# Job orders of five engines, PSUM slots and identity products of a two-layer attention and convolution kernel written anew

## The reference, cut to what matters

```python
# layer 0
attn = softmax(q @ k.T / sqrt(d) + bias)              # per 8x8 window, 4 heads
x = x + proj(attn @ v)
a, b = split(w1 @ x); g = a * sigmoid(b)
x = x + leaky(conv3x3(pad(g), w2))
# layer 1
x = x + dwconv(x, cpe1)
y = layernorm(x); act_res = silu(act @ y)
t = silu(dwconv(inp @ y, dwc))                        # nine taps per channel
q, k = elu(qk @ t) + 1; v = t
kv = rope(k).T @ v;  z = 1 / (q . mean(k))
y = rope(q) @ kv * z + dwconv(v, lepe)                # nine taps per channel
x = x + out @ (y * act_res)
x = x + dwconv(x, cpe2)
x = x + fc2 @ gelu(fc1 @ layernorm(x))
```

## Time and profile before

| | us |
|---|---|
| median of 3 runs | 854.25 |
| lowest and highest of them | 850.33, 855.42 |
| the profiled execution's own time | 852.0 |
| its span, first to last instruction | 850.2 |
| PE, DVE, ACT, POOL busy in it | 761.1, 547.1, 496.7, 299.2 |
| mean granted clock of TensorE | 0.943 of full speed |

### The profile page before, as it was taken

One profiled execution on the slowest core, in us unless ns is written; L12 is line 12 of the kernel. 1 busy time (PEld: TensorE's weight loads), 2 busy tenths in 40 slices (PEclk: granted clock), 3 DMA queues, 4 the chain that ended last, 5 costly groups with the idle time before them and its releaser, 6 DMA issues. The chain is left out here.

```text
span 850.2 us, 19878 instructions
## 1 busy us (share of the span) xinstructions
PE 761.1 (90%) x8514; PEld 478.3 (56%) x8514; DVE 547.1 (64%) x698; ACT 496.7 (58%) x675; POOL 299.2 (35%) x215
## 2 busy tenths in 40 slices
...
PEclk9899999999989996989899999999789998896999
...
GB/s 60 46 3 1 30 58 1 2 2 15 2 2 43 55 17 1 16 15 16 1 26 33 43 29 1 30 15 3 15 15 29 30 1 29 15 1 1 30 15 43
DMA packets 34345, 16.77 MB, mean 20 GB/s; under 512 B 27120, under 2 KB 34160, under 8 KB 34258
## 3 DMA queue, kind: packets, MB, share of 16 engines
...
q10 hardware_dynamic: 1808, 0.22, 0.2%
...
## 5 line engine op out<-in xcount | busy, mean ns | idle before, releaser
L1288 POOL TENSOR_TENSOR SC<-SC,mx 128x768 f32<-128x768 f32 x48 | 77.8, 1621 | 229.4 <-DVE mx L1096 229.3
L568 PE MATMUL ps<-ZP,wdw 48*64 48x384 f32 x1728 | 143.8, 483 | 1.2 <-ACT QH L990 0.8
L1163 DVE SCALAR_TENSOR_TENSOR CT<-TP,vec_sb,CT 112x768 f32<-112x768 f32 x96 | 130.2, 1368 | 1.3
L1149 DVE SCALAR_TENSOR_TENSOR QS<-ZP,vec_sb,QS 112x768 f32<-112x768 f32 x96 | 109.3, 1163 | 0.6
L568 PEld LDWEIGHTS ps<-ZP,wdw 48*64 48x64 f32 x1728 | 66.2, 133 | 72.2 <-issue 65.0
L1135 DVE TENSOR_TENSOR LV<-LV,XB 112x768 f32<-112x768 f32 x24 | 24.7, 1030 | 98.5 <-ACT LV L942 98.5
L659 PEld LDWEIGHTS ps<-vx,PT 128*128 128x128 f32 x576 | 71.6, 204 | 13.3 <-issue 5.9
L659 PE MATMUL ps<-vx,PT 128*128 128x52 f32 x576 | 74.2, 288 | 3.1 <-DVE KX L1170 1.2
L568 PE MATMUL ps<-G,w_sb 48*64 48x384 f32 x864 | 74.2, 494 | 1.9 <-ACT G L907 0.9
L815 PEld LDWEIGHTS ps<-ident_sb 128*128 128x128 f32 x534 | 64.7, 197 | 19.2 <-issue 12.2
L815 PE MATMUL ps<-ident_sb 128*128 128x128 f32 x534 | 71.2, 287 | 2.7 <-DVE XB L1221 1.4
...
## 6 DMA issues: line engine op xcount, KB each, us to landing
...
w_sb<-in_w_dram SPq DMA_DIRECT2D x2, 81.0 KB
...
wln_sb<-in_const_dram SPq DMA_DIRECT2D x6, 9.0 KB
```

The source lines that it names most:

```text
L568: mm = pe.matmul(slot(job)[half(c, HALF), r * BANK:r * BANK + SPX], w[half(r), tap * HALF:(tap + 1) * HALF], shifted(t, d * CROWS + c * WI ...
L1149: dve.scalar_tensor_tensor(out=rows16(T0[n]), in0=win, scalar=wt, in1=rows16(T0[n]), op0=ALU.mult, op1=ALU.add).then_inc(dwc_step, 1)
L1163: dve.scalar_tensor_tensor(out=ct, in0=win, scalar=wt, in1=ct, op0=ALU.mult, op1=ALU.add).then_inc(lepe_step, 1)
L1288: pool.tensor_tensor(sc, sc, bc_last(mx[:, (u % NSC) * 12:(u % NSC) * 12 + 12], TOK), ALU.subtract).then_inc(sub_ready, 1)
```

## The change

Only the five texts are replaced; no function, size, buffer or data changes. Every list holds the same jobs as before: 491 on PE, 444 on ACT, 481 on DVE, 108 on POOL, 54 on SP. Three things differ.

- The order. A job moves by 4 to 6 places on average on PE, ACT and DVE. On SP one pair of neighbours is swapped.
- The PSUM slots: 335 of the 491 jobs of PE write another slot.
- The identity products: 322 where there were 267, and at other jobs. Before `kv`, `kp`, `kk` of the last pair there are 109 (before: 91), ahead of its `kt.3.1` 20 of them, and ahead of `d3.3.0` 31 (before: 26).

The core of the diff (the ACT text and most lines of the others are left out):

```diff
--- before.py
+++ after.py
 PE_ORDER = """
...
-    v.0.0@0 v.0.1@1 s1.0.0@2+8 qk.0.0@3 sc0.0.0@0+11 sc1.0.0@1 qk.0.1@2 sc0.0.1@3+12 tr0.0.0@0+4 sc1.0.1@1
-    qk.0.2@2 tr1.0.0@0 av.0.0@0 v.0.2@3 sc0.0.2@2 ot.0.0@0 tr0.0.1@3+4 pj.0.0@1 sc1.0.2@0 qk.0.3@3 tr1.0.1@2
...
-    cv.0.2@1 qk.1.0@0 v.1.0@2 v.1.1@3 d0.0.0@1 sc0.1.0@0 sc1.1.0@2 qk.1.1@3 xc.0.0@1 d0.0.1@0 va.0.0@1 sc0.1.1@2
-    xc.0.1@3 tr1.1.0@0 d0.0.2@2 va.0.1@1 tr0.1.0@3 xc.0.2@0 ip.0.0@2 sc1.1.1@1 va.0.2@0 qk.1.2@2 ip.0.1@3
-    av.1.0@1 tr0.1.1@0 v.1.2@3 sc0.1.2@2 tr1.1.1@0 ot.1.0@1 ip.0.2@3 av.1.1@0 pj.1.0@1 v.1.3@3 tr0.1.2@2
...
-    sc0.3.5@1 v.3.5@0 kp.2.0@3 ot.3.3@2 cv.3.0@0 pj.3.3@1 tr0.3.4@2 tr1.3.4@3 sc1.3.5@0 kk.2.0@1 dn.2.0@2
...
-    f11.2.2@1 f2.2.2@3+5 kt.3.0@2 vt.3.0@1 q.3.0@0 kv.3.0@3+33 kt.3.1@1 vt.3.1@2 q.3.1@0 kt.3.2@3+17 vt.3.2@2
-    q.3.2@1 kv.3.1@0+4 kv.3.2@2+27 kp.3.0@3+6 kk.3.0@0+4 dn.3.0@1 dn.3.1@2 dn.3.2@3 at.3.0@0 at.3.1@1 at.3.2@0
-    op.3.0@2+8 op.3.1@3+6 d3.3.0@1+26 op.3.2@0 xc2.3.0@2+1 va2.3.0@3+4 f10.3.0@1+11 f11.3.0@0 d3.3.1@2 d3.3.2@3
-    xc2.3.1@1 f12.3.0@0 xc2.3.2@2 va2.3.1@3 f2.3.0@1 va2.3.2@0 f10.3.1@2+7 f12.3.1@1 f11.3.1@3 f2.3.1@0+10
-    f10.3.2@2 f12.3.2@3 f11.3.2@1 f2.3.2@0+5
...
+    v.0.0@0 v.0.1@1 s1.0.0@2+9 qk.0.0@3 sc0.0.0@0+13 sc1.0.0@1 qk.0.1@2 sc0.0.1@3+14 tr0.0.0@0+5 sc1.0.1@1
...
+    tr1.0.3@2 cv.0.0@3 sc0.0.5@2 av.0.3@0 tr0.0.4@1 tr1.0.4@3 v.0.5@2 ot.0.3@1 sc1.0.5@0 av.0.4@3 tr0.0.5@2
+    pj.0.3@1 qk.1.0@0+2 ot.0.4@2 v.1.0@3 tr1.0.5@1 pj.0.4@2 sc0.1.0@0 sc1.1.0@2 av.0.5@3 qk.1.1@1 v.1.1@0
+    tr0.1.0@2 ot.0.5@3 w1.0.3@0 pj.0.5@2 w1.0.4@3 sc0.1.1@2 sc1.1.1@1 tr1.1.0@0 w1.0.5@2 av.1.0@0 tr0.1.1@3
+    tr1.1.1@1 cv.0.1@2 ot.1.0@3 av.1.1@0 pj.1.0@1 cv.0.2@2 d0.0.0@3 ot.1.1@0 qk.1.2@1 v.1.2@2 pj.1.1@3 xc.0.0@0
+    d0.0.1@3 va.0.0@1 sc0.1.2@0 xc.0.1@2 d0.0.2@3 va.0.1@0 tr0.1.2@1 xc.0.2@2 v.1.3@3 ip.0.0@0 va.0.2@2
+    sc1.1.2@1 qk.1.3@2 ip.0.1@3 ac.0.0@1 ac.0.1@0 ip.0.2@3 ac.0.2@1 w1.1.0@3 sc0.1.3@2 sc1.1.3@0 qk.1.4@3
...
+    sc0.3.5@1 ot.3.3@2 kv.2.2@0 pj.3.3@3 sc1.3.5@2 v.3.5@1 kp.2.0@0 av.3.4@1 tr0.3.5@2 kk.2.0@0 dn.2.0@3 q.2.1@2
...
+    f2.2.2@2+12 kt.3.0@0 vt.3.0@3 q.3.0@1 kt.3.1@2+20 vt.3.1@3 q.3.1@0 kv.3.0@1 kv.3.1@2+37 kt.3.2@3 vt.3.2@1
+    q.3.2@0 kv.3.2@2+38 kp.3.0@3+8 kk.3.0@1+6 dn.3.0@0 dn.3.1@2 at.3.0@3 at.3.1@1 dn.3.2@0 at.3.2@3+7 op.3.0@2+1
+    op.3.1@1+6 d3.3.0@0+31 op.3.2@3 xc2.3.0@2+1 va2.3.0@1+4 f10.3.0@0+14 f11.3.0@3 d3.3.1@2 d3.3.2@1 xc2.3.1@0
+    f12.3.0@3 xc2.3.2@2 va2.3.1@1 f2.3.0@0 va2.3.2@3 f10.3.1@2+9 f12.3.1@0 f11.3.1@1 f2.3.1@3+12 f10.3.2@2
+    f12.3.2@0 f11.3.2@1 f2.3.2@3+6
...
 DVE_ORDER = """
...
-    sb1.1.0 sb0.1.1 yn.0.0 yn.0.1 sb1.1.1 qb.1.2 yn.0.2 c10.0.0 c11.0.0 ob.1.0 c12.0.0 sb0.1.2 c13.0.0 c10.0.1
...
-    c11.0.2 c12.0.1 sb1.1.3 c13.0.1 c12.0.2 ko.0.0 c14.0.1 ob.1.2 c15.0.1 qb.1.4 c13.0.2 qo.0.0 c14.0.2 x1.1.2
...
-    c20.2.1 c27.2.0 c21.2.1 c28.2.0 x1.3.3 c22.2.1 sb1.3.5 kk.2.0 c23.2.1 c24.2.1 c25.2.1 ob.3.4 az.2.0 c26.2.1
...
+    sb0.1.1 g.0.4 sb1.1.1 g.0.5 ob.1.0 ob.1.1 x1.1.0 qb.1.2 x1.1.1 sb0.1.2 yn.0.0 yn.0.1 sb1.1.2 yn.0.2 qb.1.3
+    c10.0.0 c11.0.0 c12.0.0 c10.0.1 c13.0.0 c11.0.1 g.1.0 c14.0.0 sb0.1.3 c15.0.0 g.1.1 c16.0.0 sb1.1.3 c17.0.0
...
+    c23.2.0 ko.2.2 qb.3.5 c24.2.0 qo.2.0 ob.3.3 c20.2.1 sb0.3.5 c21.2.1 ks.2.2 sb1.3.5 kp.2.0 x1.3.3 c22.2.1
+    ob.3.4 kk.2.0 c23.2.1 c25.2.0 c24.2.1 c26.2.0 az.2.0 x1.3.4 qo.2.1 qo.2.2 c27.2.0 c25.2.1 c28.2.0 c26.2.1
...
 POOL_ORDER = """
...
-    qs.2.1 su1.3.4 qs.2.2 su0.3.5 su1.3.5 ym.2.0 ym.2.1 ym.2.2 x2.3.0 x2.3.1 x2.3.2 kr.3.0 qc.3.0 qs.3.0 kr.3.1
-    qc.3.1 kr.3.2 qc.3.2 qs.3.1 qs.3.2 ym.3.0 ym.3.1 ym.3.2
...
+    qs.2.0 su1.3.5 qc.2.1 qc.2.2 qs.2.1 ym.2.0 qs.2.2 ym.2.1 ym.2.2 x2.3.0 x2.3.1 x2.3.2 kr.3.0 qc.3.0 kr.3.1
+    qc.3.1 qs.3.0 kr.3.2 qc.3.2 qs.3.1 qs.3.2 ym.3.0 ym.3.1 ym.3.2
...
 SP_ORDER = """
...
-    py.1.1 ld.2.2 ld.2.3 py.1.2 ld.2.4 ld.2.5 st.0.0 st.0.1 st.0.2 py.2.0 pz.1.0 pz.1.1 pz.1.2 ld.3.0 ld.3.1
...
+    py.1.1 ld.2.2 ld.2.3 py.1.2 ld.2.4 ld.2.5 st.0.0 st.0.1 st.0.2 pz.1.0 py.2.0 pz.1.1 pz.1.2 ld.3.0 ld.3.1
...
```

More of the change, by code:

```diff
@@ L72 @@
[L72 to L76, removed]
@@ L154 @@
-    c20.0.2 oz.0.1 c21.0.2 c22.0.2 c23.0.2 c24.0.2 c25.0.2 c26.0.2 c27.0.2 c28.0.2 am.0.2 oz.0.2 yn2.0.0 qb.2.0
-    sb0.2.0 yn2.0.1 sb1.2.0 qb.2.1 yn.1.0 sb0.2.1 yn.1.1 sb1.2.1 yn2.0.2 qb.2.2 yn.1.2 c10.1.0 c11.1.0 c12.1.0
-    ob.2.0 c13.1.0 sb0.2.2 c14.1.0 o.0.0 c15.1.0 x1.2.0 c16.1.0 c10.1.1 c17.1.0 sb1.2.2 c18.1.0 ob.2.1 qb.2.3
-    c11.1.1 c10.1.2 c12.1.1 c11.1.2 c13.1.1 x1.2.1 c14.1.1 sb0.2.3 ko.1.0 sb1.2.3 c15.1.1 qb.2.4 c16.1.1 ob.2.2
-    o.0.1 c17.1.1 c12.1.2 c18.1.1 sb0.2.4 x1.2.2 ks.1.0 c13.1.2 c20.1.0 c14.1.2 c21.1.0 c15.1.2 c22.1.0 ob.2.3
@@ new lines @@
+    c16.0.1 sb1.1.4 c17.0.1 qb.1.5 c18.0.1 x1.1.3 qo.0.0 g.1.2 c13.0.2 sb0.1.5 ks.0.0 c14.0.2 ko.0.1 c15.0.2
+    sb1.1.5 c16.0.2 ob.1.4 g.1.3 c17.0.2 qo.0.1 c18.0.2 c20.0.0 c21.0.0 c20.0.1 c22.0.0 ks.0.1 c21.0.1 c23.0.0
+    ko.0.2 c24.0.0 x1.1.4 qo.0.2 c22.0.1 c25.0.0 g.1.4 c26.0.0 ob.1.5 ks.0.2 c27.0.0 c23.0.1 c28.0.0 c24.0.1
+    c25.0.1 kp.0.0 c26.0.1 kk.0.0 x1.1.5 c27.0.1 c28.0.1 az.0.0 am.0.0 az.0.1 am.0.1 az.0.2 oz.0.0 g.1.5 c20.0.2
+    oz.0.1 c21.0.2 c22.0.2 c23.0.2 c24.0.2 c25.0.2 c26.0.2 c27.0.2 c28.0.2 am.0.2 oz.0.2 yn2.0.0 qb.2.0 sb0.2.0
```

187 lines of the change are left out of this document (94 added, 93 removed).

## The result

| | before | after |
|---|---|---|
| median | 854.84 us (4 runs, 850.33 to 855.69) | 874.11 us (4 runs, 865.68 to 878.03) |
| profiled execution, its span | 852.0, 850.2 | 874.4, 872.6 |
| granted clock in it | 0.943 | 0.935 |

The ratio is 1.022, with a 95% interval of 1.014 to 1.031. The kernel became slower, clear of the noise (whether by more or less than 2% the interval leaves open); the forecast was 844.2 us with a range up to 860.

The account below looks back on a forecast made before the run. It took PE to set the opening and convolution stages, DVE the stencil stages. Terms 13.0 - 11.1 - 2.8 + 0.9 - 1.8 - 1.4 - 0.9 - 3.7 = -7.8 against 852.0 gave 844.2 us, range 829 to 860.

Parts of the forecast that it names:

- Opening, +13.0: Before `c10.0.0`: 14 jobs of pair 1 moved ahead of `ip.0.1` cost their full PE time, 13.0 us more.
- Stencil stage 0, -11.1: The moved strips take 9.0 us off DVE, to 88.3, and its idle falls from 6.1 to 4: 11.1 us less.
- Stages 1 and 2, +0.9 and -1.4: Stencil stages 1 and 2: DVE gains 5.3 and 4.8 us of work, its idle falls to 3.8 and 4.1.
- The rival that DVE's waits keep their size: The three stencil stages keep 6.1, 8.2 and 10.3 us of DVE idle: 12.7 us more, 857; chance 0.20.
- Convolution stages, -2.8 and -1.8: Convolution stages 0 and 1: 2.8 us less if the slow stretch stays away, 1.8 less from exchanged jobs and fewer identity products.
- Up to `kt.3.0`, -0.9: Convolution stage 2 up to `kt.3.0`: projection and gate moved out, eight identity products more, 0.9 us less.
- Tail, -3.7: Last part: earlier `kt.3.1` ends a POOL wait and more identity products remove most slow stretches, 3.7 us less.
- The clock, 17 us of the sum: Fewer low-clock stretches in stages 0, 1, 2 and the tail: gains of 3.0, 4.4, 6.2 and 3.4 us.
- the first rival: Slow stretches only change places, so 10.8 us from stages 0, 1 and the tail are not gained: 855; no change, chance 0.22.
- Slower had 0.12: Chance given to a measured time over 862.8 us: 0.10 from the slower rival, 0.02 from the other cases.

Follow-up runs that it names:

- e6: Kernel before with eight attention jobs of pair 1 moved ahead of `ip.0.1` on PE, and 5.7 us of DVE work ahead of `c10.0.0`; 861.64 us, ratio 1.0087.
- e1: After's five lists for the opening and stencil stage 0, up to `at.0.0` on PE and `az.0.0` on DVE, then before's lists; 877.97 us, ratio 1.028 to before.
- e9: Kernel before with one DVE job, `x1.3.3`, moved earlier, to right behind `c20.2.1`; 852.81 us, ratio 0.998.
- e7: Kernel before with after's lists from the tail on, but before's counts of identity products from `d3.3.0` on; 856.01 us, ratio 1.0019.
- e11: Kernel before without the 91 identity products ahead of the last pair's `kv`, `kt.3.2`, `kp`, `kk`; 852.62 us, ratio 0.998.
- e4: Kernel after with 7 identity products added ahead of `av.0.0`; 873.69 us, ratio 1.021 to before.
- e5: Kernel after with 4 identity products added ahead of `tr0.0.1` and 4 ahead of `av.0.1`; 870.93 us, ratio 1.017 to before.
- e14: Kernel after with five PE jobs of pair 1 put back behind `ip.0.1` in one block; 888.0 us, ratio 1.038 to before.
- e15: Kernel after with five PE jobs of pair 1 put back behind `ip.0.1`, interleaved with ready work; 884.4 us, ratio 1.038 to before.

## Why the prediction was wrong, step by step

**Opening, +13.0: measured +30.5.** The price of the moved work was right: e6 moved 9.6 us and `c10.0.0` was 10.3 late. What failed is that nothing else was in the sum. No term stood for the clock, which the forecast only ever let improve; in e1 it is 6.6 us, in after's profile 14.3. That it got worse here is no chance of one profile: 18 to 40 us of low clock with after's lists, 7 to 10 with before's. Nor did a term stand for idle time (+3.8 in e1, +3.0 in after).

**Stencil stage 0, -11.1: -5.8.** DVE was to fall to 88.3 and fell to 90.0; its idle was to be 4 and is 7.6. The mis-sized term is the idle one, by 3.6 us. e1 (7.2) and e6 (7.8) show the same: less work for PE in a stage did not shorten DVE's waits.

**Stages 1 and 2, +0.9 and -1.4: -1.1 and +4.1.** In stage 2 DVE's work was forecast at 106.8 and is 106.8; the idle of 4.1 is 9.6. In stage 1 DVE got 99.7, not 104.9, and idled 7.0, not 3.8; two errors hid each other. The jobs came as counted; what shrank is the time of the 40 taps in that stage, taken as fixed. Their windows (DVE busy on the taps of the first kind, then on those of the second), before and then after:

```profile
329.20:437.00 107.80, 28.02 (x24) 0.88 0.05 12
329.20:437.00 107.80, 28.34 (x16) 0.88 0.05 12
```
```profile
347.40:454.10 106.70, 25.28 (x24) 0.92 0.04 10
347.40:454.10 106.70, 25.34 (x16) 0.92 0.04 10
```

That is 56.4 us in before and 50.6 in after for the same 40 taps, more than the 5.3 that were added. Over the three stages DVE idled 24.2 us, before 24.6, where 11.9 had been taken. The rival that DVE's waits keep their size thus held as a mechanism, and is worth the 12.3 us between the two (the rival said 12.7). The forecast's argument against it, that a good half of the idle lies in slow stretches, took a coincidence in time for a cause. The wait ahead of `kk.2.0` did go in after, and e9 shows what its going is worth alone: 0.2%, at the edge of the noise.

**Convolution stages, -2.8 and -1.8: -6.5 and +4.8.** The first had the full clock, as forecast; PE was busy 5.1 us less in it and idle 3.0 for 4.4. In the second PE idled 4.3 us for 1.9 and was busy 2.5 longer; `op.1.1` follows `am.1.1` after 8.6 us where it took 4.5. No term stood for that: the jobs at the border of two stages were counted, their distance was not.

**Up to `kt.3.0`, -0.9: -2.4. Tail, -3.7: -1.2.** `kt.3.1` did come early, and the idle of POOL ahead of `kr.3.1` went. It came back one chunk on:

```profile
762.83 1.00 POOL L1254 TENSOR_TENSOR KX<-KX,rope_th_sb 98x384 f32<-98x384 f32 x1
781.09 1.73 POOL L1254 TENSOR_TENSOR KX<-KX,rope_th_sb 98x384 f32<-98x384 f32 x1 [2.29 <-DVE KX L1169]
```

and `kv.3.2` was to be at 2.1 us by the clock; it took 4.1, at 1.2 GHz still, with 37 identity products ahead of `kv.3.1` and 38 ahead of itself (PE of after, answering to the earlier trace rows):

```profile
790.12 4.11 PE L742 MATMUL ps<-KX,VT 98*64 98x144 f32 x32 [3.62 <-issue]
813.07 7.19 PE L814 MATMUL ps<-ident_sb 128*128 128x128 f32 x62
820.75 1.52 PE L567 MATMUL ps<-ZP,wdw 48*64 48x384 f32 x16 [0.49 <-issue]
```

The 31 ahead of `d3.3.0` take 7.2 us and the wait behind them is still 0.5. `az.3.0` came 2.9 us sooner behind `kt.3.0` instead of 6.1, and 1.2 of it were left at the end.

**The clock, 17 us of the sum.** This is the largest gain that was booked and did not come. Low-clock time was read off one profile, put down to named waits, and booked as gain where these went. After has 114 us of low clock in its profile, before 97; stretches of 27.3 and 17.1 came where none over 17 had been forecast. That is the first rival, the stretches change places: its mechanism held, and its price of 10.8 left out the 6.2 of stencil stage 2. The long stretches of before do belong to its order, since they recur in eleven profiles; but where they would lie in a new order the old profile could not tell. Others can be there or not with the same jobs (e7), e11 shows that taking cover away costs nothing in the tail, and by the fit a us lost is worth 0.62.

The Trainium skill (TensorE: Matmul & The Clock Gate, section What's actually happening), on which that rival drew, holds that the count of cold products varies between runs. e7 agrees, with 0.78 for 1.00 in before's profile of the same window; the long stretches do not vary that way. Its figure of under 1% of a typical kernel's span is for the ramp penalty, and the forecast held it against the clock of the whole kernel. For that it is no bound: before loses 52.0 us, at 0.62 some 32 us, 4% of 853.

**The chances.** Slower had 0.12, and its largest case was 857, less than the 862.8 from which the forecast counts a kernel as slower. Adding that rival's 12.3 us and the opening's idle and clock of e1 (3.8 and 6.6) to 844.2 gives 867, 7 us short of the measured 874. The first was a rival, with too small a chance; the other two had no term at all.

**What stays open.** At equal clock e1 is 13.2 us over before; 5.4 (13.1 less 7.7) and 3.8 and 1.1 of idle time account for 10.3. The other 3 are not assigned, and are within what the one slope of the fit can be off. Nor is it known why the opening of after draws more low clock than before's. e1 loses 16 us more of the clock than before (68.3 for 52.0), after with the same front only 2; e4 and e5 put cover at two places and the losses were 52.9 and 46.7 for after's 54.1, but the times hardly fell. And since both undos (e14, e15) brought in waits of their own, no run shows that the moved work alone makes after slow.
